# A convolution's taps moved to VectorE, with the running sum in a PSUM bank

## The chip, the cores and the metric

The kernel runs on one core of a Trainium2 chip. The metric is the device time of one execution in microseconds (us). Median of three runs: 1773.65 us (1772.98 to 1774.02).

## The reference, cut to what matters

`x` is 8192 x 128, `adj` 8192 x 8192. All is float32.

```python
h  = relu(adj @ layernorm(x) @ gcn_w + gcn_b);  h = layernorm(h) * ln_g + ln_b
xc, z = split(h @ w_in)                                  # 256 channels each
xconv = sum(xpad[k:k+L] * conv_w[:, k] for k in range(4)) + conv_b   # 4 taps along the rows
u  = silu(xconv)
dbc = u @ w_xp;  dt = softplus(dbc[:, :8] @ w_dt + b_dt);  B, C = dbc's other 16 + 16 columns
# state of 256 x 16 numbers, row by row:  s = exp(dt * A) * s + dt * B * u;  y = s @ C
y  = (y + u * D_skip) * silu(z)
x  = x + y @ w_out
x  = x + lstm_part(layernorm(x))                         # an LSTM over the rows, cumulated sums
```

## The kernel before, in words

The 8192 rows are cut into 16 chunks of 512 (`CH`). Features lie on the 128 partitions and rows along the free dimension; the 256 inner channels are two halves (`HV`, h = 0, 1). The program of every engine is a loop of steps k = 0 to 18 (`iterations`). In step k TensorE multiplies adj for chunk k, the "pre" stage (GCN weights, layer norm, projections, convolution, dt) works on chunk k − 1, the "scan" stage on chunk k − 2 and the "post" stage on chunk k − 3. Steps 2 to 15 have adj and scan work; step 16 has pre, scan and post but no adj work; then follow two more steps, the LSTM and the output.

A step has 16 slots, and each engine's queue is written out slot by slot, in a fixed order.

- TensorE, slot s: the spread of B row s + 1 into `b_bank` (L430), two adj matmuls (each recorded as two rows, L493), the spread of C row s, two adj matmuls. Into this go the steps of the table `SHARED` (L70), which all use one PSUM bank, `shared` (bank 2): a step with slot 4 stands ahead of the adj work of slot 4, one with 4.5 in its middle. Each waits until the step before it in the table has been read out of the bank (`shared_read`), since there is only this one bank. xc0 and xc1 project the convolution's input, z0 and z1 the gate; dbc, dt0, dt1 and out follow.
- VectorE, slot s (L1078): side work (`side_part`), then dbu for state s + 1 (L1046, `make_dbu`), the scans of state s, one per half (L1093), and then the product of the scanned state s − 1 with its C row (L1054, `make_hc`), unless that state is in `POOL_HC`. A dbu waits for its spread and for the scan of two states before it; a scan waits for ScalarE's exponential and for the product of the state two before it, since the buffers are double.
- ScalarE, slot s: for a state of `POOL_HC` first a copy of its C row to SBUF (L710, GpSimd can't read the bank; there is one such buffer), then the two exponentials for the scan of state s (L733), each waiting for the same half's scan of state s − 1; then the copy of the last state column (L715), then `pre_part` and `post_part`.
- GpSimd, slot s: the product of state s − 1 where it is in `POOL_HC` (L873), then the addition of the product of state s − 1 into `acc` (L858). In step 16 and after GpSimd makes all products and TensorE adds them.

The convolution before: in slot 4 ScalarE copies xc0 and xc1 out of the bank into `xc` (L638) and makes the first product with the bias into `wd` (L628); in slots 4 to 6 it makes the other three taps' products (`tap`, L631) into `wa`, `wb`, `wc`; GpSimd adds them to `wd` in slots 5, 6 and 7 (`add_tap`, L821), 128x1024 each. ScalarE copies z0 and z1 in slot 5 (L649) and takes the silu of `wd` in slot 8.

Of the kernel before, what the change touches and what calls it, by code (L numbers as in the profile page):

```python
# [24 lines left out]
CH = 512  # L25
# [9 lines left out]
HV = DI // P  # L35
DS = 16
TAPS = 4
HALO = TAPS - 1
DR = 8
BC = 2 * DS  # L40
# [23 lines left out]
for _n, _s in VSIZE.items():  # L64
# [2 lines left out]
VTOT = _o  # L67


SHARED = [("gcn", 0, "pre"), ("cen", 1, "pre"), ("var", 2, "pre"), ("xc0", 4, "pre"), ("xc1", 4.5, "pre"),  # L70
          ("z0", 5, "pre"), ("z1", 5.5, "pre"), ("dbc", 9, "pre"), ("dt0", 10, "pre"), ("dt1", 10.5, "pre"),
          ("out", 11.5, "post"), ("pcen", 12.5, "post"), ("pvar", 13.5, "post")]
POOL_HC = (3, 8, 10)
PRE_STEPS = sum(s[2] == "pre" for s in SHARED)
POST_STEPS = sum(s[2] == "post" for s in SHARED)

# [1 line left out]
def shared_index(step, k, pre, post):  # L78

    if isinstance(k, int):  # L80
        before = PRE_STEPS * (min(k, NC + 1) - 1) + POST_STEPS * max(0, k - 3)
    else:
        before = (PRE_STEPS + POST_STEPS) * k - (PRE_STEPS + 3 * POST_STEPS)
    names = [s[0] for s in SHARED if (pre and s[2] == "pre") or (post and s[2] == "post")]
    return before + names.index(step)
# [18 lines left out]
def wait(eng, sem, value):  # L104

    if not (isinstance(value, int) and value <= 0):
        eng.wait_ge(sem, value)
# [11 lines left out]
def build(nc, adj_t, x_rows, x_t, weights, vectors, lstm_bias, out_t):  # L119
    F32, BF, I32 = mybir.dt.float32, mybir.dt.bfloat16, mybir.dt.int32  # L120
    ALU, ACT, AX = mybir.AluOpType, mybir.ActivationFunctionType, mybir.AxisListType
# [5 lines left out]
    with ctx:  # L127
# [3 lines left out]
        def sem(name):  # L131
            return ctx.enter_context(nc.semaphore(name))
# [52 lines left out]
        dbc, r1 = carve(CH), carve(CH)  # L185
# [39 lines left out]
        def V(name, i=0):  # L225
            return v_sb[:, VOFF[name] + i:VOFF[name] + i + 1]
# [17 lines left out]
        def sems(names):  # L244
            return [sem(n) for n in names.split()]
# [13 lines left out]

        squared, ln_ready, rstd_ready, h_ready = sems("squared ln_ready rstd_ready h_ready")  # L260
        cen_ready, pool_hc_done = sems("cen_ready pool_hc_done")
        halo_ready, tap_ready, tap_done, u_ready, sz_ready = sems("halo_ready tap_ready tap_done u_ready sz_ready")
        high_ready, r1_ready, mid_rounded, mid_ready, low_ready = sems("high_ready r1_ready mid_rounded mid_ready low_ready")
        pos_dt, exp_dt, one_dt, log_dt = sems("pos_dt exp_dt one_dt log_dt")
# [314 lines left out]
        def _(act):  # L579
# [22 lines left out]
            def step(k, par, adj, pre, scan, post):  # L602
                cs, q = k - 2, 1 - par

                def written(name):
                    act.wait_ge(shared_written, shared_index(name, k, pre, post) + 1)

                def pre_part(s):
# [13 lines left out]
                        act.wait_ge(shared_read, shared_index("var", k, pre, post) + 1)  # L622
                        nc.scalar.activation(ht, ht, ACT.Identity, bias=V("ln_b"), scale=V("ln_g")).then_inc(h_ready, 1)

                    def tap(i, dest):
                        for h in range(HV):
                            if i == 0:
                                last = nc.scalar.activation(dest[:, h, :], xc[q][:, h, i:i + CH], ACT.Identity,  # L628
                                                            bias=V("conv_b", h), scale=V("conv_w", h * TAPS + i))
                            else:  # L630
                                last = nc.scalar.activation(dest[:, h, :], xc[q][:, h, i:i + CH], ACT.Copy,  # L631
                                                            scale=V("conv_w", h * TAPS + i))
                        last.then_inc(tap_ready, 1)

                    if s == 4:
                        for h in range(HV):
                            written(f"xc{h}")
                            nc.scalar.activation(xc[q][:, h, HALO:HALO + CH], shared[:, :], ACT.Copy).then_inc(shared_read, 1)  # L638
                        act.wait_ge(shared_read, shared_index("xc1", k, pre, post) + 1)
                        act.wait_ge(halo_ready, k)  # L640
                        tap(0, wd)
                    if s == 5:
                        tap(1, wa)
                        nc.scalar.activation(xc[1 - q][:, :, 0:HALO], xc[q][:, :, CH:CH + HALO], ACT.Copy).then_inc(halo_ready, 1)
                        if post:
                            act.wait_ge(y_ready, k - 2)
                        for h in range(HV):
                            written(f"z{h}")
                            nc.scalar.activation(sz[q][:, h, :], shared[:, :], ACT.Copy).then_inc(shared_read, 1)  # L649
                    if s == 6:  # L650
                        tap(2, wb)
                        tap(3, wc)
                    if s == 8:
                        act.wait_ge(tap_done, HALO * k)
                        nc.scalar.activation(u[q], wd, ACT.Silu).then_inc(u_ready, 1)
                        act.wait_ge(shared_read, shared_index("z1", k, pre, post) + 1)
                        nc.scalar.activation(sz[q], sz[q], ACT.Silu).then_inc(sz_ready, 1)
                        act.preload_act_table_set(LN_EXP)
# [140 lines left out]
        def _(pool):  # L799
# [12 lines left out]
            def step(k, par, adj, pre, scan, post):  # L812
                cs, q = k - 2, 1 - par

                def add_tap(s):

                    i = s - 4
                    pool.wait_ge(tap_ready, TAPS * (k - 1) + (i + 1))
                    if i > 1:
                        pool.wait_ge(tap_done, HALO * (k - 1) + (i - 1))  # L820
                    nc.gpsimd.tensor_tensor(out=wd, in0=wd, in1=(wa, wb, wc)[i - 1], op=ALU.add).then_inc(tap_done, 1)  # L821

                def pre_part(s):
                    if drains(k):
                        return
# [57 lines left out]
                for s in range(16):  # L883
                    if post and s == 0:
                        post_part(s)
                    if scan and not drains(k) and s >= 1 and s - 1 in POOL_HC:
                        make_hc(s - 1)
                    if pre and s in (5, 6, 7):
                        add_tap(s)
                    if scan and drains(k):  # L890
                        make_hc(s)
                    elif scan and s >= 2:
                        add(s - 1)
                    if pre:
                        pre_part(s)
                    if post and s > 0:
                        post_part(planned(k, s, "post"))
# [16 lines left out]
        def _(dve):  # L914
# [60 lines left out]
            def step(k, par, adj, pre, scan, post):  # L975
                cs, q = k - 2, 1 - par

                def written(name):
                    dve.wait_ge(shared_written, shared_index(name, k, pre, post) + 1)

                def side_part(slot):
# [11 lines left out]
                    if pre and s == 3:  # L993
                        dve.wait_ge(rstd_ready, k)
                        nc.vector.tensor_tensor(out=ht, in0=ht, in1=shared[:, :], op=ALU.mult).then_inc(shared_read, 1)
                    if pre and s == 10:
                        dve.wait_ge(high_ready, k)
                        nc.vector.tensor_tensor(out=r1[0:PARTS * BC, :], in0=dbc[0:PARTS * BC, :], in1=bc_parts[q][:, :],
                                                op=ALU.subtract).then_inc(r1_ready, 1)
# [270 lines left out]
```

## Time and profile before

| | us |
|---|---|
| median of 3 runs | 1773.65 |
| the profiled execution | 1775.21 |
| its span in the trace | 1773.4 |
| VectorE busy | 1508.7 |
| TensorE busy (matmuls are pipelined) | 1593.0 |
| ScalarE busy | 1046.8 |
| GpSimd busy | 1027.3 |

The span is the time from the first to the last instruction in the trace. Busy time counts an engine's own instructions; what an engine waits for is read from the rows of other views. PE is TensorE's matmuls, PEld its weight loads, DVE VectorE, ACT ScalarE, POOL GpSimd.

### The profile page before, as it was taken

How to read it: one execution, taken by the hardware profiler on the slowest of the kernel's cores; microseconds unless marked ns; L12 is line 12 of the kernel's file. 1: busy time of each engine (PE TensorE's matmuls, PEld its weight loads, DVE VectorE, ACT ScalarE, POOL GpSimd, SP SyncE). 2: the span in 40 equal slices, each digit the busy share in tenths (PEclk: the TensorE clock that was granted, in tenths of full speed). 3: DMA queues.
4: the chain of work that ended last, by engine and by line, in shares of the span. 5: the costliest groups of instructions: out<-in, count | busy, mean ns of one | idle time of the engine just before them, and what ended most of it. 6: DMA issues, size and time to landing. Idle time of an engine off the chain costs nothing. (4 is left out here: it accounts for less than half of the span.)

```text
span 1773.4 us, 21077 instructions
## 1 busy us (share of the span) xinstructions
PE 1593.0 (90%) x5362; PEld 801.5 (45%) x5362; DVE 1508.7 (85%) x1636; ACT 1046.8 (59%) x2092; POOL 1027.3 (58%) x446
## 2 busy tenths in 40 slices
PE   6999999999999999999999999999565679999963
PEld 2444344444344444434344444434222249989940
DVE  8418999999999999999999999999989955545579
ACT  3245676757666675757666675757554446656643
POOL 3034878778888877878887877878754520000012
PEclk9999999999999999999999999999888889999975
DMA  8976665666566575666566576665002020000002
GB/s 318 333 258 233 220 216 208 234 232 222 206 218 243 169 270 214 216 231 222 219 202 247 180 260 227 211 235 181 12 0 89 6 93 8 0 1 0 0 0 95
DMA packets 52093, 298.32 MB, mean 168 GB/s; under 512 B 5532, under 2 KB 5544, under 8 KB 19112
## 3 DMA queue, kind: packets, MB, share of 16 engines
q1 hardware_dynamic: 49680, 293.30, 46.7%
q10 hardware_dynamic: 2328, 4.21, 0.6%
q14 instruction: 71, 0.58, 0.1%
q8 instruction: 14, 0.23, 0.1%
HBM read 285.69 MB, written 11.80 MB: 168 GB/s over the span
## 5 line engine op out<-in xcount | busy, mean ns | idle before, releaser
L493 PE MATMUL bank<-ring,xh 128*128 128x512 f32 x2048 | 955.7, 595 | 14.1 <-DVE xh L943 13.6
L858 POOL TENSOR_TENSOR work<-work 128x1024 f32<-128x1024 f32 x210 | 517.1, 2463 | 238.8 <-DVE work L1054 232.5
L493 PEld LDWEIGHTS bank<-ring,xh 128*128 128x128 f32 x2048 | 389.1, 191 | 458.5 <-issue 424.0
L1093 DVE TENSOR_TENSOR_SCAN work<-bank,hstate,work 128x512 f32<-128x512 f32 x448 | 548.9, 1265 | 1.3
L733 ACT ACTIVATE bank<-work,a_neg 128x512 f32<-128x512 f32 x448 | 302.1, 688 | 264.8 <-DVE work L1093 264.5
L1046 DVE TENSOR_TENSOR work<-work,bank 128x1024 f32<-128x1024 f32 x256 | 309.5, 1214 | 52.7 <-PE bank L430 39.1
L430 PE MATMUL bank<-bc_parts,sel 96*128 96x512 bf16 x512 | 192.9, 388 | 27.1 <-DVE work L1054 25.8
L1054 DVE TENSOR_TENSOR work<-work,bank 128x1024 f32<-128x1024 f32 x182 | 216.2, 1194 | 0.0
L425 PE MATMUL bank<-work,w_sb 128*128 128x512 f32 (+2 forms) x352 | 184.4, 621 | 27.5 <-ACT work L649 10.3
L908 POOL TENSOR_TENSOR ring<-work,ring 128x512 f32 (+1 forms) x16 | 17.8, 1113 | 307.3 <-DVE ring L1204 305.4
L821 POOL TENSOR_TENSOR work<-work 128x1024 f32<-128x1024 f32 x48 | 116.0, 2417 | 79.7 <-ACT work L631 79.6
L518 PE MATMUL bank<-ring,w_sb 128*128 (+1 forms) x1024 | 137.2, 278 | 0.0
L528 PE MATMUL bank<-xh,w_sb 128*128 (+1 forms) x1008 | 134.1, 276 | 0.8 <-DVE xh L1125 0.8
L430 PEld LDWEIGHTS bank<-bc_parts,sel 96*128 96x128 bf16 x512 | 50.6, 99 | 184.5 <-issue 104.1
L873 POOL TENSOR_TENSOR work<-work,xh 128x1024 f32<-128x1024 f32 x32 | 80.0, 2501 | 84.7 <-DVE work L1093 49.5
L518 PEld LDWEIGHTS bank<-ring,w_sb 128*128 128x128 f32 x1024 | 127.1, 195 | 2.2 <-issue 0.7
L528 PEld LDWEIGHTS bank<-xh,w_sb 128*128 128x128 f32 x1008 | 123.5, 193 | 1.2 <-DVE xh L1125 1.2
L1093 DVE TENSOR_TENSOR_SCAN work<-xh,hstate,work 128x512 f32<-128x512 f32 x64 | 117.5, 1875 | 0.0
L459 PE MATMUL bank<-work,xh 128*128 128x512 f32 x128 | 79.3, 754 | 41.4 <-POOL work L873 34.5
L425 PEld LDWEIGHTS bank<-work,w_sb 128*128 128x128 f32 (+2 forms) x352 | 61.5, 189 | 116.9 <-issue 56.7
L1118 DVE TENSOR_TENSOR work<-work 128x256 f32<-128x256 f32 x128 | 54.5, 425 | 53.0 <-ACT work L765 52.7
L873 POOL TENSOR_TENSOR work<-work 128x1024 f32<-128x1024 f32 x42 | 99.3, 2364 | 0.0
(138 smaller groups left out, 1571.2 us busy)
## 6 DMA issues: line engine op xcount, KB each, us to landing
ring<-adj_t SPq DMA_DIRECT2D x256, 1024.0 KB, 4.9
xh<-x_rows SPq DMA_DIRECT2D x16, 256.0 KB, 6.7
work<-x_t SPq DMA_DIRECT2D x16, 256.0 KB, 4.7
x_scratch<-work ACTq DMA_DIRECT2D x16, 256.0 KB, 5.5
work<-x_scratch SPq DMA_DIRECT2D x1, 4096.0 KB, 13.7
out_t<-ring SPq DMA_DIRECT2D x16, 256.0 KB, 2.3
xl_scratch<-work SPq DMA_DIRECT2D x13, 256.0 KB, 2.2
ring<-xl_scratch SPq DMA_DIRECT2D x1, 3328.0 KB, 12.0
```

The costliest lines, as they stand in the source:

```text
L425: last = nc.tensor.matmul(out, a, b, start=(n == 0), stop=(n == len(ins) - 1))
L430: nc.tensor.matmul(bank_[n % 2][:, :], sel[:, row * P:(row + 1) * P], bc_parts[par][:, :], start=True, stop=True).then_inc(ready, 1)
L493: last = nc.tensor.matmul(mixed[:, :], xn[:, j, :], a, start=(j == 0), stop=(j == BLK - 1))
L518: last = nc.tensor.matmul(g[:, q * HS:(q + 1) * HS], W("w_ih", q * D, (q + 1) * D), xls[:, b * (NC // 2):(b + 1) * (NC // 2), bass.ds(t * ...
L528: last = nc.tensor.matmul(g[:, q * HS:(q + 1) * HS], W("w_hh", q * D, (q + 1) * D), hs[:, t, b * HS:(b + 1) * HS], start=False, stop=(q == ...
L733: nc.scalar.activation(da_drain[s % 2][h] if drains(k) else da[h], dt[par][:, h, :], ACT.Exp, scale=a_neg[:, h * DS + s:h * DS + s + 1]).t ...
L821: nc.gpsimd.tensor_tensor(out=wd, in0=wd, in1=(wa, wb, wc)[i - 1], op=ALU.add).then_inc(tap_done, 1)
L858: nc.gpsimd.tensor_tensor(out=acc, in0=hc[0] if n == 1 else acc, in1=hc[n % 2], op=ALU.add).then_inc(y_added, 1)
L873: nc.gpsimd.tensor_tensor(out=hc[n % 2], in0=hb[n % 2], in1=c.unsqueeze(1).broadcast_to([P, HV, CH]), op=ALU.mult).then_inc(pool_hc_done, 1)
L1046: nc.vector.tensor_tensor(out=dbu[n % 2], in0=dtu[par], in1=both(b_bank[n % 2]), op=ALU.mult).then_inc(dbu_done, 1)
L1054: nc.vector.tensor_tensor(out=hc[n % 2], in0=hb[n % 2], in1=both(c_bank[n % 2]), op=ALU.mult).then_inc(hc_done, 1)
L1093: nc.vector.tensor_tensor_scan(hb[s % 2][:, h, :], da_drain[s % 2][h] if drains(k) else da[h], dbu[s % 2][:, h, :], hstate[:, HV * s + h:H ...
```

## The change

The first product with the bias is written by ScalarE back into the bank `shared`, in place of the projection. VectorE then runs three `scalar_tensor_tensor` instructions for each half: each multiplies a shifted slice of `xc` by its tap's weight and adds the bank; the first two write the bank, the last one `wd`. Each waits for the one before it, and after the last VectorE increments `tap_done` by itself. Half 0 stands at the head of VectorE's slot 5, half 1 at the head of slot 6. The bank counts as read only with the last tap. GpSimd's `add_tap` and ScalarE's three other products go. xc1 moves from slot 4.5 to 5.5, z0 from 5 to 6.5, z1 from 5.5 to 7; ScalarE's copy of xc1 and its first product move to slot 5, the copy of the halo columns to slot 6, the copies of z0 and z1 to slot 7. `POOL_HC` is (2, 4, 6, 8, 10) in place of (3, 8, 10), so that the products of states 2, 4 and 6 go from VectorE to GpSimd and that of state 3 the other way.

```diff
--- before.py
+++ after.py
@@ -35,6 +35,7 @@
 HV = DI // P
 DS = 16
 TAPS = 4
+TAPS_DONE = 6
 HALO = TAPS - 1
 DR = 8
 BC = 2 * DS
@@ -67,10 +68,10 @@
 VTOT = _o
 
 
-SHARED = [("gcn", 0, "pre"), ("cen", 1, "pre"), ("var", 2, "pre"), ("xc0", 4, "pre"), ("xc1", 4.5, "pre"),
-          ("z0", 5, "pre"), ("z1", 5.5, "pre"), ("dbc", 9, "pre"), ("dt0", 10, "pre"), ("dt1", 10.5, "pre"),
+SHARED = [("gcn", 0, "pre"), ("cen", 1, "pre"), ("var", 2, "pre"), ("xc0", 4, "pre"), ("xc1", 5.5, "pre"),
+          ("z0", 6.5, "pre"), ("z1", 7, "pre"), ("dbc", 9, "pre"), ("dt0", 10, "pre"), ("dt1", 10.5, "pre"),
           ("out", 11.5, "post"), ("pcen", 12.5, "post"), ("pvar", 13.5, "post")]
-POOL_HC = (3, 8, 10)
+POOL_HC = (2, 4, 6, 8, 10)
 PRE_STEPS = sum(s[2] == "pre" for s in SHARED)
 POST_STEPS = sum(s[2] == "post" for s in SHARED)
 
@@ -259,6 +260,7 @@
 
         squared, ln_ready, rstd_ready, h_ready = sems("squared ln_ready rstd_ready h_ready")
         cen_ready, pool_hc_done = sems("cen_ready pool_hc_done")
+        xc_ready = sem("xc_ready")
         halo_ready, tap_ready, tap_done, u_ready, sz_ready = sems("halo_ready tap_ready tap_done u_ready sz_ready")
         high_ready, r1_ready, mid_rounded, mid_ready, low_ready = sems("high_ready r1_ready mid_rounded mid_ready low_ready")
         pos_dt, exp_dt, one_dt, log_dt = sems("pos_dt exp_dt one_dt log_dt")
@@ -622,36 +624,26 @@
                         act.wait_ge(shared_read, shared_index("var", k, pre, post) + 1)
                         nc.scalar.activation(ht, ht, ACT.Identity, bias=V("ln_b"), scale=V("ln_g")).then_inc(h_ready, 1)
 
-                    def tap(i, dest):
-                        for h in range(HV):
-                            if i == 0:
-                                last = nc.scalar.activation(dest[:, h, :], xc[q][:, h, i:i + CH], ACT.Identity,
-                                                            bias=V("conv_b", h), scale=V("conv_w", h * TAPS + i))
-                            else:
-                                last = nc.scalar.activation(dest[:, h, :], xc[q][:, h, i:i + CH], ACT.Copy,
-                                                            scale=V("conv_w", h * TAPS + i))
-                        last.then_inc(tap_ready, 1)
-
-                    if s == 4:
-                        for h in range(HV):
-                            written(f"xc{h}")
-                            nc.scalar.activation(xc[q][:, h, HALO:HALO + CH], shared[:, :], ACT.Copy).then_inc(shared_read, 1)
-                        act.wait_ge(shared_read, shared_index("xc1", k, pre, post) + 1)
-                        act.wait_ge(halo_ready, k)
-                        tap(0, wd)
-                    if s == 5:
-                        tap(1, wa)
+                    if s in (4, 5):
+                        h = s - 4
+                        written(f"xc{h}")
+                        nc.scalar.activation(xc[q][:, h, HALO:HALO + CH], shared[:, :], ACT.Copy).then_inc(xc_ready, 1)
+                        act.wait_ge(xc_ready, HV * (k - 1) + h + 1)
+                        if h == 0:
+                            act.wait_ge(halo_ready, k)
+                        nc.scalar.activation(shared[:, :], xc[q][:, h, 0:CH], ACT.Identity,
+                                             bias=V("conv_b", h), scale=V("conv_w", h * TAPS)).then_inc(tap_ready, 1)
+                    if s == 6:
+                        wait(act, tap_done, TAPS_DONE * (k - 1))
                         nc.scalar.activation(xc[1 - q][:, :, 0:HALO], xc[q][:, :, CH:CH + HALO], ACT.Copy).then_inc(halo_ready, 1)
+                    if s == 7:
                         if post:
                             act.wait_ge(y_ready, k - 2)
                         for h in range(HV):
                             written(f"z{h}")
                             nc.scalar.activation(sz[q][:, h, :], shared[:, :], ACT.Copy).then_inc(shared_read, 1)
-                    if s == 6:
-                        tap(2, wb)
-                        tap(3, wc)
                     if s == 8:
-                        act.wait_ge(tap_done, HALO * k)
+                        act.wait_ge(tap_done, TAPS_DONE * k)
                         nc.scalar.activation(u[q], wd, ACT.Silu).then_inc(u_ready, 1)
                         act.wait_ge(shared_read, shared_index("z1", k, pre, post) + 1)
                         nc.scalar.activation(sz[q], sz[q], ACT.Silu).then_inc(sz_ready, 1)
@@ -812,14 +804,6 @@
             def step(k, par, adj, pre, scan, post):
                 cs, q = k - 2, 1 - par
 
-                def add_tap(s):
-
-                    i = s - 4
-                    pool.wait_ge(tap_ready, TAPS * (k - 1) + (i + 1))
-                    if i > 1:
-                        pool.wait_ge(tap_done, HALO * (k - 1) + (i - 1))
-                    nc.gpsimd.tensor_tensor(out=wd, in0=wd, in1=(wa, wb, wc)[i - 1], op=ALU.add).then_inc(tap_done, 1)
-
                 def pre_part(s):
                     if drains(k):
                         return
@@ -885,8 +869,6 @@
                         post_part(s)
                     if scan and not drains(k) and s >= 1 and s - 1 in POOL_HC:
                         make_hc(s - 1)
-                    if pre and s in (5, 6, 7):
-                        add_tap(s)
                     if scan and drains(k):
                         make_hc(s)
                     elif scan and s >= 2:
@@ -993,6 +975,19 @@
                     if pre and s == 3:
                         dve.wait_ge(rstd_ready, k)
                         nc.vector.tensor_tensor(out=ht, in0=ht, in1=shared[:, :], op=ALU.mult).then_inc(shared_read, 1)
+                    if pre and s in (5, 6):
+                        h = s - 5
+                        dve.wait_ge(tap_ready, HV * (k - 1) + h + 1)
+                        for i in range(1, TAPS):
+                            if i > 1:
+                                dve.wait_ge(tap_done, TAPS_DONE * (k - 1) + HALO * h + (i - 1))
+                            nc.vector.scalar_tensor_tensor(
+                                out=wd[:, h, :] if i == TAPS - 1 else shared[:, :], in0=xc[q][:, h, i:i + CH],
+                                scalar=V("conv_w", h * TAPS + i), in1=shared[:, :], op0=ALU.mult,
+                                op1=ALU.add).then_inc(shared_read if i == TAPS - 1 else tap_done, 1)
+                            if i == TAPS - 1:
+                                dve.wait_ge(shared_read, shared_index(f"xc{h}", k, pre, post) + 1)
+                                dve.sem_inc(tap_done, 1)
                     if pre and s == 10:
                         dve.wait_ge(high_ready, k)
                         nc.vector.tensor_tensor(out=r1[0:PARTS * BC, :], in0=dbc[0:PARTS * BC, :], in1=bc_parts[q][:, :],
```

## Rows read from the trace of the kernel before

**Rows 1.** The page, part 1: busy us, share of the span and instructions.
```profile
PE 1593.0 (90%) x5362; PEld 801.5 (45%) x5362; DVE 1508.7 (85%) x1636; ACT 1046.8 (59%) x2092; POOL 1027.3 (58%) x446
```

**Rows 2.** Window of one chunk: busy us (and instructions) of five engines, clock, DMA.
```profile
614.80:693.90 79.10, 75.88 (x190) 31.92 (x189) 76.70 (x67) 51.29 (x92) 62.77 (x28) 1.00 0.63 222
```

**Rows 3.** Groups by line, VectorE, that chunk: shapes, count | busy, ns | idle before.
```profile
L1093 DVE TENSOR_TENSOR_SCAN work<-bank,hstate,work 128x512 f32<-128x512 f32 x32 | 39.2, 1265 | 0.1
L1046 DVE TENSOR_TENSOR work<-work,bank 128x1024 f32<-128x1024 f32 x16 | 19.3, 1214 | 3.0 <-PE bank L430 1.6 <-POOL work L837 1.1
```

**Rows 4.** Timeline, VectorE: start us, duration us, engine, line, operation [idle before].
```profile
633.01 1.19 DVE L1054 TENSOR_TENSOR work<-work,bank 128x1024 f32<-128x1024 f32 x1
634.13 1.21 DVE L1046 TENSOR_TENSOR work<-work,bank 128x1024 f32<-128x1024 f32 x1
...
637.81 1.22 DVE L1046 TENSOR_TENSOR work<-work,bank 128x1024 f32<-128x1024 f32 x1
...
641.46 1.19 DVE L1054 TENSOR_TENSOR work<-work,bank 128x1024 f32<-128x1024 f32 x1
644.29 1.22 DVE L1046 TENSOR_TENSOR work<-work,bank 128x1024 f32<-128x1024 f32 x1 [1.63 <-PE bank L430]
...
653.52 1.21 DVE L1046 TENSOR_TENSOR work<-work,bank 128x1024 f32<-128x1024 f32 x1
...
668.13 1.21 DVE L1046 TENSOR_TENSOR work<-work,bank 128x1024 f32<-128x1024 f32 x1
```

**Rows 5.** Timeline, TensorE, slots 4 to 6 of that chunk.
```profile
634.48 1.12 PE L425 MATMUL bank<-work,w_sb 128*128 128x512 f32 x2 [0.52 <-ACT work L638]
635.44 0.38 PE L430 MATMUL bank<-bc_parts,sel 96*128 96x512 bf16 x1
...
637.38 0.38 PE L430 MATMUL bank<-bc_parts,sel 96*128 96x512 bf16 x1
...
643.87 0.38 PE L430 MATMUL bank<-bc_parts,sel 96*128 96x512 bf16 x1
```

**Rows 6.** Waits of VectorE, 218 to 1249 us: us in total, times, longest.
```profile
DVE work L1046 <- PE bank L430: 21.3, 13, 1.6
```

**Rows 7.** Timeline, VectorE: the first dbu of the first and last adj chunk.
```profile
138.27 2.35 DVE L1046 TENSOR_TENSOR work<-work,bank 128x1024 f32<-128x1024 f32 x2 [11.45 <-PE bank L430]
...
1249.31 1.22 DVE L1046 TENSOR_TENSOR work<-work,bank 128x1024 f32<-128x1024 f32 x1
```

**Rows 8.** One line each, VectorE, 512 columns: duration in ns, min/median/max.
```profile
L995 DVE TENSOR_TENSOR work<-work,bank x16: 654/677/686, 84.4 to 1269.8; 128x512 f32<-128x512 f32 x16
...
L1204 DVE SCALAR_TENSOR_TENSOR ring<-work,v_sb x16: 719/721/736, 1714.7 to 1757.3; 128x512 f32 x14, 128x512 f32<-128x512 f32 x2
...
L1181 DVE SCALAR_TENSOR_TENSOR work<-bank,work,xh x16: 1079/1094/1107, 1710.1 to 1754.3; 128x512 f32<-128x512 f32 x16
```

**Rows 9.** Timeline, VectorE: an instruction that waits for the one before it.
```profile
70.34 0.27 DVE L965 TENSOR_TENSOR bias_in<-bias_in 4x128 f32<-4x128 f32 x1
70.64 0.21 DVE L966 CAST bias_mid<-bias_in 4x128 bf16<-4x128 f32 x1
```

**Rows 10.** Timeline, GpSimd, slot 2 of that chunk.
```profile
629.16 2.36 POOL L858 TENSOR_TENSOR work<-work 128x1024 f32<-128x1024 f32 x1 [4.54 <-DVE work L1054]
```

**Rows 11.** Timeline, ScalarE, slot 4 of that chunk.
```profile
633.13 0.69 ACT L733 ACTIVATE bank<-work,a_neg 128x512 f32<-128x512 f32 x1 [0.48 <-DVE work L1093]
...
633.85 0.57 ACT L638 ACTIVATE work<-bank 128x512 f32<-128x512 f32 x1
```

**Rows 12.** Timeline, VectorE, the chunk without adj work.
```profile
1262.65 2.45 DVE L1093 TENSOR_TENSOR_SCAN work<-xh,hstate,work 128x512 f32<-128x512 f32 x2
...
1274.69 1.22 DVE L1046 TENSOR_TENSOR work<-work,bank 128x1024 f32<-128x1024 f32 x1
...
1295.01 5.55 DVE L1093 TENSOR_TENSOR_SCAN work<-xh,hstate,work 128x512 f32<-128x512 f32 x2
1300.67 1.22 DVE L1046 TENSOR_TENSOR work<-work,bank 128x1024 f32<-128x1024 f32 x1
```

## The prediction, made before the changed kernel was run

> **What bounds the kernel now.** The page gives busy shares, but they mix stages [rows 1], so I read one chunk of the long stage by itself. The first dbu of the first and the last chunk with adj and scan work stand 1111.04 us apart, which is 14 chunks of 79.36 us [rows 7]. In such a chunk VectorE is busy 76.70 of 79.10 us, TensorE 75.88, GpSimd 62.77 and ScalarE 51.29, at the full granted clock (1.00, the 2.4 GHz level) [rows 2]. VectorE is the limit, and its groups say where its idle time lies: 1.6 us before a dbu, for TensorE, and 1.1 for GpSimd [rows 3]. The 1.6 us wait recurs: 13 times, 21.3 us [rows 6]. Its place is the dbu of slot 6, idle 1.63 us [rows 4], until TensorE's spread at 643.87 [rows 5]. TensorE was late there because four projections through one bank lie in slots 4 to 5.5, and it waited 0.52 us for ScalarE to empty the bank behind xc0 [rows 5]; behind z0 the same thing happens again. So what an edit is worth is what it adds to VectorE's queue, plus what it does to this wait.
>
> **Off VectorE.** The products of states 2, 4 and 6 go to GpSimd and that of 3 comes back: two fewer. One costs its start to the next start, 633.01 to 634.13 = 1.12 us [rows 4]. Without it the next dbu waits for the scan that has just ended: a slot with the product takes 641.46 − 637.81 plus 1.12 = 4.77 us where it too began with a late scan, and one without takes 637.81 − 634.13 = 3.68, of which about 0.1 is that late start [rows 4]. Before, one such slot had no side work to cover this 0.1; after, two (slots 4 and 8). Saved: 2 × 1.12 − 0.1 = 2.1 us a chunk.
>
> **On VectorE.** Six taps of 128x512 per chunk. The trace has no VectorE instruction that writes a bank, so I bound one. From below: the add with one input in the same bank, 0.68 us. Next: a scalar_tensor_tensor with a column of v_sb, 0.72. From above: a scalar_tensor_tensor that reads a bank, 1.09, though that one also permutes its input and compares [rows 8]. A tap is nearest to the first two: 0.70. Each waits for the one before it. A waiting instruction starts 0.03 us after the end of its predecessor's row [rows 9], where an unhindered one starts 0.08 before it (634.13 against 633.01 + 1.19 [rows 4]). Three taps are 3 × 0.73 = 2.2 us, and with the separate increment behind the last, about 0.05 by the same row, 2.25. Two halves: 4.5 us a chunk. Bounds for a tap's pitch: 0.60 (0.68 less the overlap) and 1.12. VectorE's own work grows by 4.5 − 2.1 = 2.4 us.
>
> On the wait itself the Trainium skill says otherwise (VectorE: DVE Perf Modes, section "The DRAIN you can't avoid"): a semaphore after each VectorE instruction costs nothing extra, since the next one starts only when the pipe is empty. The trace disagrees by the 0.11 us between the two starts just named. By that rule six taps would cost 0.6 us a chunk less, 9 us in all.
>
> **What the new waits do.** I walk the chunk of rows 4 with the new order.
> 1. Slot 4: without the product of state 2 its dbu starts at 633.2 (scan ended at 633.1, as ScalarE's waiting exponential at 633.13 shows [rows 11]). GpSimd makes that product behind its add at 629.16 [rows 10]: 629.16 + 2.36 + 2.36 = 633.9, before scan 4 needs it at 634.3. dbu 1.13, scans 2.37, product of state 3 1.12: 637.8.
> 2. Slot 5: taps of half 0 to 640.05. Their first sum lies ready: ScalarE had xc0 copied at 634.42 [rows 11] and writes the product one activation later. Behind this wait stand dbu 6 and scan 5, so nothing is lost. dbu and scans with no product: 643.55. TensorE's xc1 now waits for these taps (to 640.1 instead of 634.48). That eats its lead and no more: xc1 0.96, spread 0.22, a half slot 1.72 [rows 5] put the spread of b 7 at 643.1, and dbu 7 wants it only at 645.8.
> 3. Slot 6: taps of half 1 to 645.8 (ScalarE's first sum is there at about 642.7), dbu, scans to 649.4. Before, the same scans ended at 644.29 + 1.13 + 2.45 = 647.9. So here the chunk is only 1.5 us late: the old wait of 1.63 has gone.
> 4. It comes back at slot 8. z1 is now at the head of slot 7 and waits for ScalarE's copy of z0, which stands in ScalarE's queue behind the exponentials of slot 7, and these wait for scan 6. Rows of before have this very path: scan 3 ended 633.10, copy ended 634.42, TensorE started 634.48, so 1.38 us [rows 5, 11]. From z1 to a dbu behind the next spread: 0.96 + 1.72 + 0.22 + 1.72 + 0.42 = 5.04 (0.42 is 644.29 − 643.87). dbu 9 starts at 649.4 + 1.4 + 5.04 = 655.8; VectorE would be there at 649.3 + 1.12 + 1.13 + 2.47 = 654.1. New wait 1.7.
> 5. From there TensorE has dbc, dt0, dt1 and out before it: a plain slot takes it 2 × 1.94 = 3.88 (0.22 and 1.72 twice) and each extra matmul 0.86. Its spread of b 12 comes 3 × 3.88 + 4 × 0.86 = 15.08 after that of b 9, at 670.5, and dbu 12 at 670.9. VectorE's own way from dbu 9 to dbu 12 is 668.13 − 653.52 = 14.61 [rows 4], so it waits 0.5 more. Behind slot 12 TensorE catches up, and the chunk's end, GpSimd's chain to dtu, is as before.
> The chunk is late by 670.9 − 668.13 = 2.8 us. Fourteen chunks: 39 us.
>
> **The chunk without adj work.** There all scan operands lie in SBUF and GpSimd makes every product. Two scans take 2.45 us beside an idle GpSimd and 5.55 beside its product and a tap's addition [rows 12]. From dbu 5 to dbu 9 now 1300.67 − 1274.69 = 26.0 us [rows 12]. After: the additions are gone, the taps read only one operand from SBUF (the product in the long stage does too, and keeps 1.19 us beside a busy GpSimd), and GpSimd's products of slots 4 and 5 run beside taps. Slots 5 and 6 then take 1.13 + 2.45 each. Slots 4 and 7 have one product beside their scans; the 3.1 us that two GpSimd operations add bound it between 0 and 3.1, and I take a third, 1.1: 4.7 each. Sum 2 × 3.6 + 2 × 4.7 + 2 × 2.25 = 21.1. Gain 5 us, bounds 1 and 7. The first chunk of this work has no scan; nothing there waits for taps: 0. ScalarE loses six passes a chunk and gains two copies of C, all in idle time: 0. No DMA moves.
>
> **Sum.** Against the profiled execution, 1775.21 us: 1775.2 + 39 − 5 = 1809. The median shown is 1.6 lower, so I forecast 1808.
>
> **Rivals.**
> - *Taps at the upper bound.* Writing and reading one bank could make each cost 1.09: 6 × 0.39 = 2.3 us a chunk more, 33 in all: 1841. For it: no row has such a write. Against: only a permuted input costs that much.
> - *The waits on TensorE vanish.* Spreading the four projections over slots 4 to 7 was all that was needed, and z0's copy is early enough. Then the chunk pays 2.4 − 1.6 = 0.8: 14 × 0.8 − 5 = +6: 1780. Against: step 4's path in ScalarE's queue.
> - *The same, with taps at their lower pitch, 0.60* (the other side). VectorE's six taps then take 3.6, less 2.1 saved and 1.6 of idle time filled: −0.1 a chunk, with the 5 us of the last chunk −6: 1767. It decides when all of the old wait is filled and a tap is under about 0.62.
> - *GpSimd is the limit* (faster as well). It loses three additions and gains two products, 2.36 us a chunk: 14 × 2.36 + 5 = 38: 1736. For it: the 1.1 us before dtu. Against: it is idle 16 us a chunk [rows 2], and that wait is set in slots 12 to 15, which keep their work.
> - *The clock.* With TensorE waiting some 5 us a chunk, it could fall to its 1.2 GHz level for a few us here and there; a chunk that loses 1.7 us by it makes 1832.
>
> **How the numbers follow.** Forecast 0.61, dear taps 0.12, clock 0.04, waits vanish 0.14, filled idle time with cheap taps 0.05, GpSimd 0.02, the rest 0.02 near no change. The range holds the second rival and reaches the first: 1778 to 1842. A measurement of this kernel tells about 0.2% (3.5 us) from no change: faster 0.07, same 0.04, slower 0.89.
>
> **What would show it.** Taps near 0.70 us with starts 0.73 apart; VectorE's wait of 1.63 before dbu 7 gone and one of about 1.7 before dbu 9, on the spread; TensorE waiting at xc1 and z0 for VectorE and at z1 for ScalarE's copy; chunk pitch 82.2 us; the slots 4 to 7 of the chunk without adj in 21 us. Wrong if dbu 9 starts without a wait, or if a tap's row is far from 0.70.

## The result, and the profile after

The changed kernel takes 1824.13 us (median of 4 runs, 1821.39 to 1824.48) against 1773.84 us for the kernel before beside it (1772.98 to 1774.51). The ratio is 1.028, 95% interval 1.0263 to 1.0298: 50 us slower. The profiled execution took 1824.03 us, its span 1822.3.

The page's first part answers to [rows 1]: VectorE 29 us busier, GpSimd 49 and ScalarE 33 less.

```profile
PE 1596.5 (88%) x5362; PEld 805.2 (44%) x5362; DVE 1537.7 (84%) x1704; ACT 1013.7 (56%) x2024; POOL 978.6 (54%) x426
```

The first dbu of the first and of the last chunk with adj work answer to [rows 7]:

```profile
139.31 1.22 DVE L1041 TENSOR_TENSOR work<-work,bank 128x1024 f32<-128x1024 f32 x1 [11.40 <-PE bank L432]
...
1302.26 1.22 DVE L1041 TENSOR_TENSOR work<-work,bank 128x1024 f32<-128x1024 f32 x1
```

Fourteen chunks now take 1162.95 us, 83.07 each, where [rows 7] gave 1111.04 and 79.36: +51.9 us. The chunk without adj work takes from its first dbu to the next chunk's 97.98 us instead of 102.34, −4.4; the first dbu is 1.0 later. Together +48.5 of the 48.9 us between the two spans. So the loss lies in the long stage alone.

VectorE in slots 4 to 8 of the chunk that starts at 635.6 us answers to [rows 4]; the columns are the same:

```profile
657.45 1.19 DVE L1049 TENSOR_TENSOR work<-work,bank 128x1024 f32<-128x1024 f32 x1
658.57 1.54 DVE L984 SCALAR_TENSOR_TENSOR bank<-work,v_sb,bank 128x512 f32<-128x512 f32 x2
660.14 0.75 DVE L984 SCALAR_TENSOR_TENSOR work<-work,v_sb,bank 128x512 f32<-128x512 f32 x1
661.19 1.22 DVE L1041 TENSOR_TENSOR work<-work,bank 128x1024 f32<-128x1024 f32 x1 [0.30 <-DVE work L984]
...
664.70 1.52 DVE L984 SCALAR_TENSOR_TENSOR bank<-work,v_sb,bank 128x512 f32<-128x512 f32 x2
666.25 0.75 DVE L984 SCALAR_TENSOR_TENSOR work<-work,v_sb,bank 128x512 f32<-128x512 f32 x1
667.31 1.22 DVE L1041 TENSOR_TENSOR work<-work,bank 128x1024 f32<-128x1024 f32 x1 [0.31 <-DVE work L984]
...
679.01 1.22 DVE L1041 TENSOR_TENSOR work<-work,bank 128x1024 f32<-128x1024 f32 x1 [3.51 <-PE bank L432]
```

Three taps stand in front of the dbu of slot 5 (661.19) and three in front of that of slot 6 (667.31); the first tap starts at 658.57, so a group takes 2.62 us. 0.30 of it is idle time behind the last tap. The old wait of 1.63 before dbu 7 is gone. In its place VectorE waits before dbu 9, here 3.51 us.

TensorE in slots 5 to 8 answers to [rows 5]:

```profile
660.94 1.13 PE L427 MATMUL bank<-work,w_sb 128*128 128x512 f32 x2 [2.36 <-DVE work L984]
...
667.06 1.12 PE L427 MATMUL bank<-work,w_sb 128*128 128x512 f32 x2 [1.12 <-DVE work L984]
...
672.28 1.61 PE L427 MATMUL bank<-work,w_sb 128*128 128x512 f32 x2 [1.95 <-ACT work L644]
673.68 3.14 PE L495 MATMUL bank<-ring,xh 128*128 128x512 f32 x4
676.66 0.38 PE L432 MATMUL bank<-bc_parts,sel 96*128 96x512 bf16 x1
...
678.60 0.38 PE L432 MATMUL bank<-bc_parts,sel 96*128 96x512 bf16 x1
```

It waits 2.36 us at xc1 and 1.12 at z0, both for VectorE's last tap, and 1.95 at z1 for ScalarE's copy. That copy answers to [rows 11]: it starts at 671.65, behind an exponential that starts at 670.93, when scan 6 has ended.

```profile
670.93 0.69 ACT L725 ACTIVATE bank<-work,a_neg 128x512 f32<-128x512 f32 x1 [0.48 <-DVE work L1088]
...
671.65 0.58 ACT L644 ACTIVATE work<-bank 128x512 f32<-128x512 f32 x1
```

The four records of two adj matmuls at 673.68 take 3.14 us where the others here take 1.88. Windows of one chunk and of the place itself answer to [rows 2] (busy us of the five engines, granted clock, DMA share, GB/s):

```profile
303.30:385.50 82.20, 76.45 (x192) 32.55 (x191) 78.54 (x71) 50.28 (x89) 61.19 (x27) 1.00 0.60 214
635.60:719.50 83.90, 77.28 (x189) 32.64 (x188) 78.55 (x71) 49.21 (x88) 60.35 (x27) 0.98 0.59 210
671.50:675.50 4.00, 3.21 (x5) 1.42 (x6) 4.00 (x4) 1.91 (x5) 3.33 (x2) 0.66 0.60 236
```

Around z1 the granted clock is at its lower level for a part of the time (0.66 in the mean of 4 us). Four chunks earlier in the stage it is not, and dbu 9 waits 1.81 us, not 3.51:

```profile
345.00 1.22 DVE L1041 TENSOR_TENSOR work<-work,bank 128x1024 f32<-128x1024 f32 x1 [1.81 <-PE bank L432]
```

The trace has six such low stretches in the 14 chunks, where the kernel before had one. Five lie at z1, and each of these five chunks is 1.7 us longer than one at the full clock (these alternate, but for the first two and the last, between 82.2 and 83.0 to 83.1 us, as they did between 79.0 and 79.8 before).

The taps themselves answer to [rows 8]: 0.75 us, and those that write the bank (x64) cost what the one that writes SBUF costs (x32).

```profile
L984 DVE SCALAR_TENSOR_TENSOR bank<-work,v_sb,bank x64: 723/754/756, 92.5 to 1339.0; 128x512 f32<-128x512 f32 x64
L984 DVE SCALAR_TENSOR_TENSOR work<-work,v_sb,bank x32: 748/748/748, 94.1 to 1339.8; 128x512 f32<-128x512 f32 x32
```

### The profile page after: what moved, and what is told of

Read it like the earlier page. It is cut to its first block and busy times, and to the rows that moved or that the text cites. A ratio compares the mean times of both kernels' runs of the same rounds, so it can differ in the third digit from the quotient of the medians.

```text
span 1822.3 us, 21210 instructions
## 1 busy us (share of the span) xinstructions
PE 1596.5 (88%) x5362; PEld 805.2 (44%) x5362; DVE 1537.7 (84%) x1704; ACT 1013.7 (56%) x2024; POOL 978.6 (54%) x426
## 5 line engine op out<-in xcount | busy, mean ns | idle before, releaser
L842 POOL TENSOR_TENSOR work<-work 128x1024 f32<-128x1024 f32 x210 | 516.8, 2461 | 320.6 <-DVE work L1049 311.1
L1041 DVE TENSOR_TENSOR work<-work,bank 128x1024 f32<-128x1024 f32 x256 | 310.2, 1217 | 75.9 <-PE bank L432 53.5
L1049 DVE TENSOR_TENSOR work<-work,bank 128x1024 f32<-128x1024 f32 x154 | 182.9, 1195 | 0.0
L857 POOL TENSOR_TENSOR work<-work 128x1024 f32<-128x1024 f32 x70 | 165.2, 2359 | 1.3 <-POOL work L842 0.3
L1088 DVE TENSOR_TENSOR_SCAN work<-xh,hstate,work 128x512 f32<-128x512 f32 x64 | 109.7, 1753 | 0.0
L814 POOL TENSOR_TENSOR work<-work 128x1024 f32<-128x1024 f32 x15 | 35.4, 2360 | 107.3 <-DVE work L997 107.3
```

The costliest lines, as they stand in the source:

```text
L842: nc.gpsimd.tensor_tensor(out=acc, in0=hc[0] if n == 1 else acc, in1=hc[n % 2], op=ALU.add).then_inc(y_added, 1)
L857: nc.gpsimd.tensor_tensor(out=hc[n % 2], in0=hb[n % 2], in1=c.unsqueeze(1).broadcast_to([P, HV, CH]), op=ALU.mult).then_inc(pool_hc_done, 1)
L1041: nc.vector.tensor_tensor(out=dbu[n % 2], in0=dtu[par], in1=both(b_bank[n % 2]), op=ALU.mult).then_inc(dbu_done, 1)
L1049: nc.vector.tensor_tensor(out=hc[n % 2], in0=hb[n % 2], in1=both(c_bank[n % 2]), op=ALU.mult).then_inc(hc_done, 1)
L1088: nc.vector.tensor_tensor_scan(hb[s % 2][:, h, :], da_drain[s % 2][h] if drains(k) else da[h], dbu[s % 2][:, h, :], hstate[:, HV * s + h:H ...
```

## The experiments

Each was timed beside the kernel before on the same chip. "Pitch" is the mean time of the 14 chunks, from the first dbu of the first chunk to that of the chunk without adj work, as in [rows 7], in one profiled execution of each kernel. Low stretches of the clock are counted in the same execution.

| kernel | median us | ratio to before, 95% | pitch us |
|---|---|---|---|
| before (1773.8 to 1775.5 in the comparisons) | 1773.8 | | 79.36 |
| changed | 1824.1 | 1.0263 to 1.0298 | 83.07 |
| products only | 1784.6 | 1.0039 to 1.0072 | 80.19 |
| taps only | 1844.3 | 1.0344 to 1.0418 | 84.46 |
| last tap only | 1780.1 | 1.0017 to 1.0038 | 79.93 |
| no own increment | 1808.1 | 1.0174 to 1.0208 | 81.89 |
| repeated spread | 1815.3 | 1.0199 to 1.0245 | 82.45 |
| z1 half a slot later | 1793.5 | 1.0087 to 1.0120 | 80.89 |
| both repairs | 1788.6 | 1.0038 to 1.0088 | 80.42 |
| before, z0 and z1 later | 1751.4 | 0.9850 to 0.9882 | 77.73 |
| the same, five products | 1810.0 | 1.0185 to 1.0226 | 81.68 |
| the same, state 1 as well | 1745.2 | 0.9812 to 0.9845 | 77.24 |

My theory was the prediction's step 4: the chunk's length is set by one path, VectorE up to scan 6, ScalarE's copy of z0, z1 on TensorE, and the spread of b 9. The rival was that VectorE's sum of work decides.

**Products only.**

```diff
 (in the kernel before)
-POOL_HC = (3, 8, 10)
+POOL_HC = (2, 4, 6, 8, 10)
```

> The kernel before with POOL_HC = (2, 4, 6, 8, 10) alone; taps stay on ScalarE and GpSimd, the table of shared steps stays. Theory 'VectorE's queue': VectorE loses two products, 2.1 us a chunk, but the wait for the spread of b 7 in slot 6 (1.6 us) grows by what is saved ahead of it, since TensorE is late there by its own queue; two of the three moved products lie ahead of slot 6, so only some 1 us a chunk is won: about 1760 us. Rival 'GpSimd's slots': in slots 5 to 7 GpSimd now has an addition, a tap's addition and every second slot a product, 2.4 us each, against 3.7 to 4.7 us a slot, and VectorE comes to wait for products 4 and 6: 1 to 3 us a chunk slower, 1790 to 1815.

Measured 1784.6: slower, though VectorE does 2 products less a chunk. Neither size was right, and the loss has two causes. VectorE's waits and one of ScalarE's (us in all, times, longest):

```profile
DVE work L1046 <- PE bank L430: 48.3, 26, 3.4
DVE work L1093 <- ACT bank L733: 28.7, 13, 2.2
```
```profile
ACT work L655 <- POOL work L821: 19.8, 13, 1.5
```

Of waits of VectorE for GpSimd's products there is none. The wait for a spread grew from 21.3 us [rows 6] to 48.3, and one for ScalarE's exponential is new. ScalarE now copies the C row of state 4 as well (L710, 0.48 us from its start to the next instruction's), ahead of its copy of z0; TensorE waits 1.11 us at z1 where it waited 0.63, and dbu 7 comes 0.48 us later in the chunk than in the kernel before, though dbu 5 comes 0.93 earlier. The other cause is GpSimd's slots after all, by a way that neither theory named: the taps' additions now stand behind the products of states 4 and 6, ScalarE's silu (L655) waits for the last of them up to 1.5 us, and the exponentials of slot 9 stand behind the silu, so that scan 9 waits 2.2 us. The products' move by itself loses, because part of the saved time lies ahead of a wait and the added work lies on two paths to VectorE.

**Taps only.**

```diff
 (in the changed kernel)
-POOL_HC = (2, 4, 6, 8, 10)
+POOL_HC = (3, 8, 10)
```

> The changed kernel with POOL_HC = (3, 8, 10) as before: the taps alone. VectorE has two products more than in the changed kernel, 2.1 us a chunk. Theory 'scan 6 to z0's copy to z1': only what lies ahead of scan 6 counts. Products 2 and 4 come back ahead of it and product 3 goes, so +1.1 us a chunk, and product 6 falls into the wait before dbu 9, which shrinks by 1.1: 1824 + 15 = about 1839. Rival 'VectorE's sum of work': every product counts, +2.1 us a chunk: about 1853.

Measured 1844.3, between the two. The chunks that a low clock doesn't lengthen decide: the fifth, which has no low stretch, takes 83.1 us and in the changed kernel 82.2; the first three, whose low stretch lies ahead of z1, take 82.9, 82.9 and 83.1 against 82.0, 82.0 and 82.2. So +0.9 for two products more, near the path's 1.1 and not 2.1 (dbu 5 comes 0.93 later too, and the later ones no more than that). That is 13 of the 20 us. The rest is the clock: 13 low stretches in this trace, 9 of them at z1, 4 more than in the changed kernel.

**Last tap only.**

```diff
 (in the changed kernel, tap_done now counts 2 a chunk)
-                        for i in range(1, TAPS):
-                            if i > 1:
-                                dve.wait_ge(tap_done, ...)
+                        for i in range(TAPS - 1, TAPS):
```

> The changed kernel with only the last of the three taps of each half on VectorE (taps 1 and 2 are left out of the computation): four of six instructions go. In the trace a tap's start to the next is 0.78 us. Theory 'scan 6 to z0's copy to z1': all four stand ahead of scan 6, the whole path shifts by 4 x 0.78 = 3.1 us a chunk, and the low-clock stretches at z1 become fewer as TensorE waits less: 1824 - 44 = 1780, down to 1772. Rival 'waits take it back': TensorE's own queue limits once the taps are short, the wait before dbu 9 or 12 grows by up to 1 us a chunk: about 1794.

Measured 1780.1, as the theory said; this kernel leaves out two taps of each half, so it only prices them. The first two chunks take 78.8 us against 82.0: 3.2 us for four taps, 0.8 each, and in other chunks at the full clock dbu 9 comes 2.8 to 3.2 us earlier. So all or nearly all of a tap's time is on the path. Four low stretches behind z1 are left, of five, so of fewer low stretches little came.

**No own increment.**

```diff
 (in the changed kernel, tap_done now counts 4 a chunk)
-                            if i == TAPS - 1:
-                                dve.wait_ge(shared_read, shared_index(f"xc{h}", k, pre, post) + 1)
-                                dve.sem_inc(tap_done, 1)
...
-                        act.wait_ge(tap_done, TAPS_DONE * k)
+                        act.wait_ge(shared_read, shared_index("xc1", k, pre, post) + 1)
 (ScalarE's wait for tap_done ahead of the copy of the halo columns goes too)
```

> The changed kernel without VectorE's wait and its own increment of tap_done behind each half's last tap; ScalarE's silu waits for shared_read of xc1 instead. The dbu behind the taps starts 0.30 us after the last tap's end in the changed kernel. Theory: the 0.30 (and the 0.08 of overlap) goes, 2 x 0.35 us a chunk on the path to scan 6: 10 us less, 1814. Rival: the idle 0.30 is the wait for the last tap's write itself, which dbu needn't have, or it is made up by the later waits: 1820 or more.

Measured 1808.1, 16 us less. VectorE's timeline shows the dbu directly behind the last tap (0.08 before its row's end):

```profile
654.78 0.75 DVE L983 SCALAR_TENSOR_TENSOR work<-work,v_sb,bank 128x512 f32<-128x512 f32 x1
655.45 1.21 DVE L1037 TENSOR_TENSOR work<-work,bank 128x1024 f32<-128x1024 f32 x1
```

A group takes 655.45 − 653.21 = 2.24 us and no longer 2.62. Chunks take 81.8 and 82.3 to 82.4 us against 82.2 and 83.0, the first two 81.4 against 82.0: dbu 8 comes 0.8 us earlier in most of them, all of the saving, and about 0.57 of the 0.76 reach the chunk's end, 8 us in all; the rest is lost at the head of the next chunk, where its first dbu waits 0.69 us for GpSimd in every other chunk instead of 0.34. The other 8.5 us: in this trace no low stretch of the clock makes dbu 9 wait longer than 1.81 us, although there are seven. So of the expected 10 us the increment gave 8, and the clock gave as much again, which the expectation did not have.

**Repeated spread.**

```diff
 (in the changed kernel, TensorE, ahead of the spread of b 8)
+                    if n == 8 and adj:
+                        for _ in range(5):
+                            nc.tensor.matmul(b_bank[n % 2][:, :], sel[:, n * P:(n + 1) * P],
+                                             bc_parts[par][:, :], start=True, stop=True)
```

> The changed kernel with the spread of b 8 made six times over (same data, same bank, ready after the last) in the chunks with adj work: 5 x 0.22 = 1.1 us of TensorE work put into its wait of 1.95 us ahead of z1, before which nothing is short of it. Theory 'the waits at xc1, z0 and z1 let the clock fall': with 1.1 of about 5.4 us of waiting filled, the low-clock stretches in the adj stage (6 in the changed kernel's trace) become fewer, up to 6 x 1.7 = 10 us less: 1814 to 1824. Rival 'the clock falls for another reason' (power, or the waits at slots 5 and 6): as many low stretches, 1824 or a little more.

Measured 1815.3: 9 us less with more work for TensorE. Its wait for ScalarE's copy is 0.9 us at most:

```profile
PE bank L427 <- ACT work L648: 9.7, 13, 0.9
```

All chunks take 82.0 to 82.2 or 83.0 to 83.2 us, the changed kernel's lengths without a low clock; dbu 9 waits 1.81 us in every one of them. But five low stretches remain, elsewhere in the chunks, where TensorE is ahead and they cost nothing. So it was only half as I expected: what vanished is not the low stretches but their place behind z1.

**z1 half a slot later.**

```diff
 (in the changed kernel; in SHARED)
-          ("z0", 6.5, "pre"), ("z1", 7, "pre"),
+          ("z0", 6.5, "pre"), ("z1", 7.5, "pre"),
 (ScalarE: the copy of z1 moves from slot 7 to the head of slot 8's work)
```

> The changed kernel with z1 half a slot later (7.5 in place of 7) and its copy at the head of ScalarE's work of slot 8 in place of slot 7; nothing else. Theory 'scan 6 to z0's copy to z1': by slot 7.5 z0's copy is done, TensorE doesn't wait at z1, and the wait before dbu 9 (1.8 us, or 3.5 where the granted clock is at its lower level just there) goes to nearly nothing: 1.5 to 2 us a chunk and most of the low-clock stretches, so 1790 to 1800. Rival 'TensorE's own queue from slot 7 on': the wait only moves to dbu 10 to 12, since TensorE has the same matmuls to do: 1815 to 1824.

Measured 1793.5: 31 us less for half a slot. VectorE's and TensorE's waits:

```profile
DVE work L1089 <- ACT bank L726: 15.0, 13, 1.2
...
DVE work L1042 <- PE bank L432: 4.3, 12, 0.4
```
```profile
PE bank L427 <- ACT work L643: 1.8, 8, 0.2
```

TensorE's wait for the copy fell from 24.9 us in the changed kernel to 1.8, and the wait before dbu 9 is gone. What is late next is new: scan 9 waits 1.2 us for ScalarE's exponential in 13 chunks, since z1's copy now stands in slot 8, ahead of the two silu and their table loads. Chunks at the full clock are 1.5 to 1.6 us shorter, some 22 us in all, and the five low stretches at z1 are gone (8.5 us; four others remain and cost nothing). Step 4 of the prediction is shown by this: its path, its place and its price.

**Both repairs.** The edits of the last experiment and of "no own increment" together.

> The changed kernel with both repairs: z1 half a slot later (alone 1793) and no increment of its own behind the taps (alone 1808). With z1 half a slot later the wait before dbu 9 is gone and VectorE has 0.35 us of idle time a chunk at two places before scan 6, a wait of 1.2 us for ScalarE's exponential before scan 9, and 0.4 before dbu 12. Theory 'one path at a time': the path to scan 9 runs through VectorE and ScalarE's slot 8, which starts from scan 7, so the 2 x 0.35 still come through, 10 us: 1783. Rival 'TensorE from slot 9 on limits already': the saving goes into the wait before dbu 12: 1790 or more.

Measured 1788.6 (1781.2 to 1792.5), between the two and with a wide scatter, so the time does not decide it. The trace says more. Against the run with z1 half a slot later, dbu 12 comes 0.8 us earlier in seven of the nine chunks that have no low stretch (0.6 in the other two), and the wait before it stays at 0.35 to 0.42 us; so the saving comes through, and the rival's wait does not grow. It is lost elsewhere: in the five chunks with a low stretch dbu 9 waits again, 0.4 to 0.7 us, and the chunk without adj work is 2.1 us longer, for a reason not looked into. The pitch fell by 0.47 us, of 0.76 saved.

**Before, z0 and z1 later.**

```diff
 (in the kernel before; in SHARED)
-          ("z0", 5, "pre"), ("z1", 5.5, "pre"),
+          ("z0", 5.5, "pre"), ("z1", 6.5, "pre"),
 (ScalarE: the copy of z0 moves to the head of slot 6's work, that of z1 to slot 7)
```

> The kernel before with z0 at slot 5.5 and z1 at 6.5 in the table of shared steps (5 and 5.5 before), their copies in ScalarE's slots 6 and 7; taps and products as before. If the wait of 1.63 us for b 7 in slot 6 comes from four projections in two slots, it goes: up to 14 x 1.6 = 22 us less, 1752. If TensorE's total is what limits, the wait moves to a later dbu and the time stays at 1774.

Measured 1751.4, faster than both kernels. The 21.3 us of [rows 6] are 0.2:

```profile
DVE work L1048 <- POOL work L839: 3.3, 8, 1.1
DVE work L1048 <- PE bank L430: 0.2, 1, 0.2
```

Pitch −1.63 us, the whole wait, and none came in its place. So in the kernel before the wait of slot 6 came from the four projections in two slots, and moving two of them was worth doing, with the taps left where they were.

**The same, five products.** In addition POOL_HC = (2, 4, 6, 8, 10).

> The kernel before with z0 at 5.5 and z1 at 6.5 (as in the run that gave 1751) and also POOL_HC = (2, 4, 6, 8, 10). The products' move alone gave 1785: there the wait for the spread of b 7 grew from 1.6 to 3.3 us. Theory: that wait was TensorE's and ScalarE's queue in slots 4 to 6 and not GpSimd; with the projections spread out the saved 2.1 us a chunk come through at least in part: 1725 to 1745. Rival 'GpSimd's slots': taps' additions and products on GpSimd hold up VectorE: 1751 or more.

Measured 1810.0, so the theory was wrong and the rival right. As in "products only", GpSimd has three taps' additions and the products in the same slots:

```profile
DVE work L1048 <- PE bank L430: 29.8, 42, 1.1
DVE work L1095 <- ACT bank L735: 26.4, 12, 2.2
DVE work L1095 <- POOL work L875: 23.9, 12, 2.0
```
```profile
ACT work L657 <- POOL work L823: 43.6, 12, 3.7
```

Scans wait for its products (23.9 us) and ScalarE's silu for its taps (43.6), longer than the 19.8 us of "products only". Chunks without a low stretch of the clock are 2.3 to 2.7 us longer than in the variant with three products, as long as those of "products only" within 0.2 us: with five products on GpSimd the later z0 and z1 gain nothing. Seven chunks have a low stretch, and six of these are 5.8 to 5.9 us longer: dbu 11 and dbu 12 wait for their spreads, and VectorE's side work of slot 12 then takes 3.3 us instead of 1.4. That makes 20 of the 55 us by which the 14 chunks grew; that the clock sets it off was not tested. In this order of steps five products on GpSimd need the taps off it.

**The same, state 1 as well.** The faster variant with POOL_HC = (1, 3, 8, 10).

> The kernel before with z0 at 5.5 and z1 at 6.5 (alone 1751) and a fourth product on GpSimd, that of state 1, in slot 2: POOL_HC = (1, 3, 8, 10). In the trace before GpSimd is idle 4.5 us just ahead of its addition of slot 2, so the product fits there and is done before scan 3. Theory 'a product moved into GpSimd's idle time is a product saved': VectorE loses 1.1 us a chunk, no wait appears: 1751 - 15 = 1736. Rival 'TensorE is now the limit': TensorE needs 75 us a chunk of 77.7 and the saving returns as waits for spreads: 1745 to 1751.

Measured 1745.2, 1.7% under the kernel before and the fastest of all, at the rival's lower end and 9 us over the theory's time. The pitch fell by 0.5 us of the 1.1 saved; a wait for a spread came back, before dbu 6, in 12 chunks:

```profile
DVE work L1048 <- PE bank L430: 9.1, 12, 1.1
```

## Why the prediction was right, and where its sizes were off

The direction and the places were right, and 1824 lies in the range (1778 to 1842); the forecast of 1808 was 16 us low. The range reached so far up for dear taps, which did not come; 8.5 of the 16 us came from the clock, which the sum had at nothing. So it is in part luck that the time lies in the range; the direction and the places are not luck, since the edits one at a time move the very waits that the walk named.

- *Two products fewer save 2.1 us, counted only where they lie ahead of scan 6.* Right: dbu 5 comes 0.93 us earlier, as the walk had it (633.2 against 634.13), and with two products more, chunks at the full clock grew by 0.9 us (taps only), not 2.1.
- *Six taps, 0.70 us each.* 0.75 were measured, and removing four saved 0.8 each. The upper bound, 1.09, was not needed: a write to the bank costs what a write to SBUF costs. A group took 2.62 us, not 2.25: 0.15 by the taps' size, the rest behind the last one, where the wait together with VectorE's own increment costs 0.30 and not 0.05 plus 0.03. That was the mis-sized term of the chunk: dbu 12 comes 3.5 us late, not 2.8. The run without the wait and the increment confirms 0.38 a group.
- *A side effect that I took as unchanged.* The side work of slot 12 (L1002 before) took 1.93 us beside GpSimd's product and now 1.31 to 1.36; it starts later within that product, which is the likely reason and was not tested. So dbu 13 is 3.2 us late where dbu 12 is 3.5: it hides about half of the 0.7 us that the dearer taps add.
- *The old wait goes, a new one of 1.7 us comes before dbu 9, and 0.5 before dbu 12.* 1.81 and 0.36 to 0.45. Shown by the half slot: without it both the wait and 31 us are gone.
- *Chunk +2.8 us.* +3.1 to 3.2 at the full clock, 43 to 44 us for fourteen where I had 39.
- *The clock.* I held it for a rival apart from the forecast, at 0.04. It came on top of it: five low stretches behind z1 at 1.7 us, 8.5 us. My price for one was right, though no row stood behind it; my chance was not, and five chunks of 14 paid it where I had all or none. That it was the place behind z1 that cost time is shown by the repeated spread.
- *The chunk without adj work: −5.* −4.4. Its two tap groups are followed by scans of 2.45 us, as the walk had them, and a group takes 2.5 us, not 2.25; slots 4 to 7, from dbu 5 to dbu 9, went from 26.0 us [rows 12] to 21.6, the two rows shown below, where I had 21.1.

Timeline of VectorE in the changed kernel, the chunk without adj work, dbu 5 and dbu 9:

```profile
1327.65 1.22 DVE L1041 TENSOR_TENSOR work<-work,bank 128x1024 f32<-128x1024 f32 x1
...
1349.23 1.22 DVE L1041 TENSOR_TENSOR work<-work,bank 128x1024 f32<-128x1024 f32 x1
```

- The rest: the stage began 1.0 us later, and the median lies 0.1 above the profiled execution where before it lay 1.4 below: 1.5 us.

By term: 16 = 8.5 (clock) + 4.4 (chunk) + 1.0 (start) + 0.6 (chunk without adj) + 1.5 (profiled execution against median).

The rule of the Trainium skill (VectorE: DVE Perf Modes, "The DRAIN you can't avoid"), that a semaphore after each instruction costs nothing, would have made a chunk's taps 0.6 us cheaper. The runs don't bear it out: in the run without the increment a tap that waits starts 0.78 us after the tap before it (half of 2.24 − 0.67) and the dbu that doesn't wait 0.67 us after a tap of the same length, 0.11 less, as the prediction read it from [rows 4] and [rows 9]; and without the wait and the increment behind the last tap the dbu starts 0.38 us earlier. How much of the 0.38 is the wait and how much the increment was not measured apart.

## What to carry to other kernels

When two engines are both nearly full, an edit's worth is not its work but what it does to the next hand-over between them: walk each queue to the instruction that will be late, and price the moved steps (here z1, half a slot too early, 31 us) as carefully as the added work. Try the edits one at a time: moving two projections alone (by half a slot and a slot, less far than in the change) gained 24 us, moving the products alone lost 9, and the taps lose even where z0 and z1 stand well in both: 1793.5 us with the taps and five products against 1751.4 without. An instruction that releases a busy bank should be followed by useful work, not by a wait for itself.

## What the runs showed of the hardware that I had not expected

- A VectorE scalar_tensor_tensor of 128x512 in float32 that reads and writes the same PSUM bank takes 0.754 us, one that reads the bank and writes SBUF 0.748.
- A wait of VectorE for its own last instruction and an increment by itself ahead of the next instruction cost 0.38 us against none (0.30 idle, 0.08 of lost overlap).
- TensorE's granted clock fell to the lower level for 3.4 us at a time six times in the 14 chunks of the changed kernel, in nearly each of which it waits 1.3 to 2.4 us at xc1, 1.1 at z0 and 1.9 at z1, 13 times with taps only (the slowest kernel), and never with products only. Why one chunk has a low stretch and another, with the same waits, has none, stays open. In the run with the repeated spread it still fell five times, but not where it delayed VectorE.
